# A new hand-placed order of pieces for a decoder layer over 32 batches: 128 pieces done ahead in place of 112, banks placed anew

## The reference

```python
x = x + attn(_layernorm(x), Wqkv, bqkv, Wout, bout)            # 16 heads, rope
x = x + xattn(_layernorm(x), ctx_1024, Wq, Wk, Wv, Wo, ...)    # 16 heads, 77 keys
x = x + ffn(_layernorm(x), ew, act_w, We, be, Wq, Wk, Wv, Wo, ln_g, ln_b)
# ffn: six attention nodes of 8 heads, one after the other
for c in range(6):
    q = ew[c,0] * (nodes[in_q] @ We[eq] + be[eq])      # in_q is the node before
    k = ew[c,1] * (nodes[in_k] @ We[ek] + be[ek])
    v = ew[c,2] * (nodes[in_v] @ We[ev] + be[ev])
    nodes[c] = act_w[c] * _mha(q, k, v, Wq[c], Wk[c], Wv[c], Wo[c]) + q
out = _layernorm(nodes[5], ln_g, ln_b)
```

## Time and profile before

| | |
|---|---|
| median of 3 runs | 5218.73 us (5194.44 to 5224.57) |
| profiled execution | 5204.53 us, its span 5202.7 us |
| PE busy | 90% of the span |
| DVE busy | 66% |
| ACT busy | 48% |
| POOL busy | 13% |
| mean granted TensorE clock | 0.963 of 2.4 GHz |
| start to row of round 0 (set-up 83.0, AHEAD 59.4) | 142.3 us |
| rounds 0 to 14 | 313.7 to 322.7 us each |
| last round | 289.3 us |

### The profile page before, as it was taken

One profiled execution on the slowest core, in us unless ns is written; L12 is line 12 of the kernel. 1 busy time (PEld: TensorE's weight loads), 2 busy tenths in 40 slices (PEclk: granted clock), 3 DMA queues, 4 the chain that ended last, 5 costly groups with the idle time before them and its releaser, 6 DMA issues.

```text
span 5202.7 us, 204839 instructions
## 1 busy us (share of the span) xinstructions
PE 4697.6 (90%) x87132; PEld 2899.1 (56%) x87132; DVE 3447.5 (66%) x5930; ACT 2485.9 (48%) x4737; POOL 671.0 (13%) x1606
## 2 busy tenths in 40 slices
...
DMA packets 43111, 48.29 MB, mean 9 GB/s; under 512 B 11552, under 2 KB 41888, under 8 KB 42144
## 3 DMA queue, kind: packets, MB, share of 16 engines
...
## 4 chain that ended last, share of the span: by engine, by line
issue 54%; PE 30%; POOL 6%; DVE 5%; ACT 1%; POOLq 1%; DVEq 0%; ACTq 0%; DMA 0%; SPq 0%
PE banks L967 15%; PE banks L961 14%; DVE row_max L927 2%; POOL neg_max L733 2%; POOL neg_max L735 2%; DVE n_tok L946 1%; POOL inv_std L706 1%; PE banks L1088 1%; POOL x_tok L712 1%; ACT probs L830 1%; DVE k_parts L899 0%; POOL var_eps L703 0%; PE banks L1018 0%; ACT n_tok L759 0%; POOL rope_c L719 0%
## 5 line engine op out<-in xcount | busy, mean ns | idle before, releaser
L927 DVE TENSOR_REDUCE row_max<-banks 128x4 f32<-128x1024 f32 (+1 forms) x1152 | 1300.3, 1169 | 327.5 <-PE banks L961 325.7
L830 ACT ACTIVATE probs<-banks 128x1024 f32<-128x1024 f32 (+1 forms) x1280 | 1138.7, 935 | 512.6 <-PE banks L961 486.1
L961 PE MATMUL banks<-k_parts,q_parts 32*128 32x256 f32 (+1 forms) x13824 | 599.5, 305 | 183.5 <-DVE row_max L927 143.1
L961 PEld LDWEIGHTS banks<-k_parts,q_parts 32*128 32x128 f32 x13824 | 482.2, 196 | 393.6 <-DVE row_max L927 184.0
L961 PE MATMUL banks<-q_parts,k_parts 32*128 32x256 f32 (+1 forms) x13824 | 600.4, 302 | 99.3 <-DVE row_max L927 63.2
L946 DVE TENSOR_TENSOR n_tok<-probs 128x512 f32<-128x512 f32 x512 | 384.8, 752 | 447.7 <-ACT probs L830 372.9
L961 PEld LDWEIGHTS banks<-q_parts,k_parts 32*128 32x128 f32 (+1 forms) x13824 | 462.4, 187 | 327.0 <-issue 117.2
L967 PE MATMUL banks<-node_t,w_n 128*32 128x256 f32 x10240 | 622.0, 381 | 4.7 <-ACT node_t L847 4.7
L733 POOL TENSOR_TENSOR neg_max<-row_max,zeros 128x8 fp32r<-128x8 f32 (+1 forms) x576 | 140.5, 244 | 3659.3 <-DVE row_max L927 3657.0
L946 DVE TENSOR_TENSOR pair_sums<-probs 128x512 f32<-128x512 f32 x512 | 369.1, 721 | 362.6 <-ACT probs L830 185.4
L840 ACT ACTIVATE context_t<-banks 128x256 f32<-128x256 f32 x512 | 197.2, 385 | 582.9 <-PE banks L961 581.1
...
## 6 DMA issues: line engine op xcount, KB each, us to landing
x_next<-in_x SPq DMA_DIRECT2D x32, 256.0 KB, 3.0
out_y<-x_tok SPq DMA_DIRECT2D x32, 256.0 KB, 2.3
w_head<-in_wf SPq DMA_DIRECT2D x11, 256.0 KB, 11.8
...
w_edge_t<-in_we_t ACTq DMA_DIRECT2D x9, 256.0 KB, 11.9
w_head<-in_wf ACTq DMA_DIRECT2D x7, 256.0 KB, 10.4
w_edge_t<-in_we_t SPq DMA_DIRECT2D x6, 256.0 KB, 10.3
w_n<-in_we ACTq DMA_DIRECT2D x3, 256.0 KB, 12.5
```

The source lines that it names most:

```text
L830: done(act.activation(probs[s][0:rows, g % 2, 2 * p:2 * p + 2, 0:kt, :] .rearrange("p c k t -> p c (k t)"), psum[0:rows, b0:b0 + 2, 0:kt * T],
L927: done(dve.reduce_max(maxima, scores, AX_X, negate=True), "max_taken", a)
L961: return nc.tensor.matmul(bank_ap, lhs, rhs, start=start, stop=stop, **kw)
```

## The change

ORDER is replaced by another row of the same 922 pieces; nothing else is edited. No instruction is added or taken out of a round. 128 pieces carry a "+" where 112 did. The 16 more are KI0.1, KH0.1, KL0.1, LNP0.1, LNN0.1, TR0.1, TRE0.1, Q0.1, QB0.1, QH0.1.0, XB0.1, KS1.0, KH1.0, KL1.0, V1.0 and VE1.0: they stood at the head of the row and stand in its tail now, so the point at which the loop jumps lies behind them. The banks are placed anew: the halves for S and ST change places at other points, and single pieces moved within their half.

```diff
@@ -145,79 +145,79 @@
 ORDER = """
-KI0.1 LNP0.1 LNN0.1 KS1.0 V1.0@3 TR0.1@4 KH0.1 KL0.1 TRE0.1 KH1.0 KL1.0 Q0.1@7 QB0.1 VE1.0 QH0.1.0 QH0.1.1
+LOADX0 QH0.1.1 QL0.1.0 QL0.1.1 S1.0.0@4 SB1.0.0 MX1.0.0.1 MX1.0.0.0 S1.0.1@0 SB1.0.1 MX1.0.1.1 MX1.0.1.0
```

145 lines of the change are left out of this document (73 added, 72 removed).

## The result

The changed kernel takes 5163.1 us (median of 5, 5161.0 to 5170.1) where the kernel before takes 5212.3 (5 runs beside it): ratio 0.991, 95% interval 0.989 to 0.993. It is faster by 0.9%, 49 us, where 2.1% and 104 us were forecast. The time lies in the range given, but within the bound of 1% that was called "within", where faster by over 1% had been the forecast.

A forecast was written before the change was run, and what follows sets the result against it. PE, busy 90% of the span, was taken as the bound, with 19 us of a round's some 29 idle ones in the seam. Terms summed to -6.9 us a round, -104 over 15 seams, giving 5108 us, range 5050 to 5192.

The forecast's parts named there:

- A: Seam from PS1.7.0 to PV0.0.2: PE's waits fall from 6.6 to 5.6 us, -1.0 us a round.
- B: Seam from PV0.0.2 to KR1.0: waits ahead of PS0.0.2 and for the context go, -1.9 us a round.
- C: KR1.0's end to first MX1.0: the jump still costs 2.85 us, what queued behind it goes, -1.9 us a round.
- D: Slot 1's maxima and start of its ST: DVE's 0.55 us waits go, MT moves ahead, -1.6 us a round.
- E: Cross attention and nodes: waits of S0.2.1 and ST0.4.1 go, small waits added elsewhere, net -0.5 us a round.
- the jump is not where I think: Rival: the jump's 2.85 us belong to something that stands still; -5.0 us a round, 5137 us, within the likeliest case's 0.56.
- slower rival: Stages 4 to 6 and 2: PE waits on DVE in six places, 5317 us; slower or no gain, chance 0.11.
- Small gain: Seam: LOADX1's load and LNP1.0, LNP1.7 come 2 us late; 3 us a round left, 5167 us, chance 0.19.
- Larger gain: After stage 1's waits: second half-clock stretch goes in all, -27 us, with -10 a round; 5035 us, chance 0.14.

The follow-up runs named there:

- jump_only: Kernel before with its row turned so the fifteen pieces KI0.1 to QH0.1.0 are done ahead of the jump, no order or bank changed; 5167.6 us, ratio 0.992.
- before_u5: Kernel before with its loop written out five rounds at a time, 3 loop ends in place of 15; 5134.5 us, ratio 0.986.
- hyb_o: Changed kernel with the first half of the seam in the kernel before's order, all S0.0.x kept in one half of the banks; 5195.2 us, ratio 0.997.
- hyb_f: Changed kernel with the first half of the seam in the kernel before's order and banks; 5160.7 us, ratio 0.990.
- after_u5: Changed kernel with its loop written out five rounds at a time, 3 loop ends in place of 15; 5136.2 us, ratio 0.986.
- after_flat: Changed kernel with its fifteen rounds written out, no loop or jump, waits for constants; 5118.6 us, ratio 0.982.
- jump_back: Changed kernel with the jump back at its old place and XB0.1 where the kernel before has it; 5230.4 us, ratio 1.004.

## Why the prediction was right or wrong, point by point

Terms by the medians, us a round (forecast, measured): A -1.0, **+1.1**; B -1.9, -1.8; C -1.9, -1.9; D -1.6, **-0.6**; E -0.5, -0.1. Before rounding the sum is -3.2 where -6.9 was said. Times 15 that is -48; the fifteen rounds of the two profiled executions differ by 43, since the changed kernel has long rounds too, the two spans by 44, and the medians of the runs by 49. So the steps that failed are A, which took 2.1 us of the 3.7 that are missing, and D, which took 1.0. Of the signs set down in the prediction, three came out against it: the round takes 314 us and not 309 to 311, the two waits of 0.55 us on DVE stayed, and PE's idle time in the seam's three stretches is 16.2 us (6.6, 4.5 and 5.1; before 19.0) and so above 15.

- **B held.** No wait for n_tok of 1.42 us (0.59 is left), none for the context.
- **C held**, in size and in kind, and jump_only shows that it is the jump's place that did it; the rival "the jump is not where I think" falls. But the term was read as idle time saved. What the jumps cost at the old place was, for two thirds, PE's work at half clock, V1.0's 3.97 us behind them and more elsewhere in the round: before_u5, idle -26, busy -50. And C was counted for 15 seams, where 14 have a jump.
- **A failed by sign.** The walk put PS1.7.0's wait at 0.6; it is 2.03. FX0 ahead of PA1.7.0.1 was seen and given no cost (0.5 measured), and FG0's hold on the first PA was taken as gone. The other waits are 4.0 us where they were 5.2 (the walk said 5.0), so all of A's waits sum to 6.0, as its sign asked (5 to 6): 0.6 us less than before. What turned the sign is the clock: 3.4 us of the stretch, on S0.0.0 and V0.0, now run at half clock, which costs 1.7, and the sum had no term for that. The bank placement, passed over as waits of 0.8 and 1.2, costs 1.2 by hyb_o and hyb_f.
- **D failed in size.** ST1.0.0 to PV1.0.0 fell by 0.9 us (said: 0.6), both MT standing ahead. First maximum to ST1.0.0 rose by 0.4 (said: -1.0): the walk gave S0.1.0 and S0.1.2 their time at full clock, and they run at half. That this kept DVE's waits of 0.55 us is argued from the rows, not shown by a run with both at full clock. In after_u5 and after_flat, too, the maxima keep 10 to 14 us at half clock.
- **E held.** S0.2.1 and ST0.4.1 pass without a wait, PV0.3.0, PV0.5.0 and PV0.6.0 wait 1.2, 1.4 and 0.9; the nodes' stretch grew by 0.5 us. The slower rival, the nodes' tight banks, did not come.
- **The premise under all five failed**: "PE's own work of 288 us in a round stays" (the figure stands in the earlier trace rows, 287.9, and the round beside it has 293.2). It is work at a clock that depends on the waits around it. The ledger has idle -60 (said -104) and busy +17 (said 0), and jump_back idle -19 and busy +51.
- **Small gain** gave the right number (5167) by luck, with a mechanism that isn't there: LOADX1 lands in 2.7 us and LNS1.0 doesn't wait for it. **Larger gain** named the half-clock stretch behind stage 1 and took for granted that less idle time could only remove it. It is hardly rarer (3 rounds in place of 4), but a new one came at S0.0.0 in every round and the one at the maxima grew from 13.7 or 17.1 to 20.5 us in most.
